# Dequantised FFN weights queued earlier in each group: ternary chunks at 3,3,3,3,3,1,0,0 and 4,4,4,4,2,2,2,0 an iteration

## The chip, the cores and the metric

The kernel runs on the eight cores of one Trainium2 chip. Each core works on eight of the 32 query tiles of one of two batch rows; no core waits for another. Times are device microseconds of the slowest core.

## The reference

One layer: a normalised input goes through a squared-score linear attention and, in parallel, through a feed-forward block whose weights are ternary. Only the second is touched here:

```python
def weight_quant(w):
    scale = 1.0 / jnp.clip(jnp.mean(jnp.abs(w)), 1e-05, None)
    return jnp.clip(jnp.round(w * scale), -1, 1) / scale
def bit_linear(x, w, g):
    xn = rms_norm(x, g)
    xq = ste(xn, activation_quant(xn))
    wq = ste(w, weight_quant(w))
    return xq @ wq.T
y = bit_linear(x, gate_w, gate_norm_w)       # 2048 -> 2 x 5632
gate, up = jnp.split(y, 2, axis=-1)
h = gate * jax.nn.sigmoid(gate) * up
return bit_linear(h, down_w, down_norm_w)    # 5632 -> 2048
```

The output is the input plus the attention plus this block.

## The kernel before

The kernel runs in stages: normalisation and the key, value and query products; the attention; the output product of the attention (L813); the gate/up product; a requantisation of the hidden values; the down product. Between stages all engines meet at a barrier. The change touches the gate/up stage and the down stage.

Weights arrive as float32 and are turned into -1, 0 and 1 on the core, chunk by chunk. A chunk is 128 x 1024 values. `tern_ld` loads two chunks with one DMA of 1 MB on GpSimd's (POOL's) queue into one of two `wfpt` slots; the load waits until both chunks that were last in the slot have been read. `tern_sc` makes a chunk by two signs on ScalarE (L741, L744) and an add on VectorE (L747); its first sign waits for the add of the previous such chunk, since all share `sgn0` and `sgn1`. `tern_dve` makes a chunk on VectorE alone, by two compares and a subtraction (L754, L757, L760).

The gate/up stage has 11 groups `g` of 512 columns and in each 8 row tiles `s`. A group needs 16 chunks, eight for `terng` by `tern_sc` and eight for `ternu` by `tern_dve`, taken alternately. Both weight tiles have two rings: while group g is multiplied, group g+1's chunks are made. In the order of the program, an iteration first queues its chunks (`emit_tern`), then the load of `xqs` for the iteration after next on SyncE (three slots), then 16 matmuls into `gps` (L892) and 16 into `ups` (L904), each over three PSUM slots. After them come the silu on ScalarE (L912), the product `kg2` on VectorE (L916), a square with sum on ScalarE (L921), its accumulation (L925), the weighting (L930), a maximum (L934, L936) and, on SyncE, the store of `hgb` to `hgscr`. `emit_tern(n, max_g=g+1)` stops at the end of group g+1. The first matmul of a group waits for the last chunk of that group; the first chunk of group g+1 waits for the last matmul of group g-1, whose ring it writes.

The down stage has four column blocks `m` of 512 and eight row tiles `s` in each. A block needs 22 chunks, all by `tern_sc`; the chunks of block m+1 are made during block m, those of block 0 in the stage before. An iteration queues its chunks (`emit_dtern`), the load of the next `hqts` (two slots, 1.4 MB) and of `xob` on SyncE, 44 matmuls into `dps` (L1118, two PSUM slots), two steps on VectorE (L1128, and L1134, which reads `xob`), and the store of `outb` on SyncE. The load of `hqts` for s+2 so stands on SyncE's queue behind the store of s.

Every engine works its own instructions off in program order, and the helpers `V` and `SC` make each VectorE and ScalarE instruction also wait for the one before it on its engine.

Of the kernel before, what the change touches and what calls it, by code (L numbers as in the profile page):

```python
# [100 lines left out]
def build_nc():  # L101
# [59 lines left out]
    def SC(fn, waits=(), drain=True):  # L161
        w = list(waits) + ([(cS, cS.n)] if drain else [])
        return b.op("scalar", fn, waits=w, inc=cS)

    def TE(fn, waits=(), inc=True):
        return b.op("tensor", fn, waits=waits, inc=(cT if inc else None))
# [605 lines left out]
    def emit_tern(n, max_g=99):  # L772
        for _ in range(n):
            if tq_i[0] >= len(tern_q):
                return
            kind, g, ring, f2 = tern_q[tq_i[0]]
            if g > max_g:
                return
            tq_i[0] += 1
            extra = [(cT, tern_free[ring])] if (kind == "sc" and f2 == 0) or \  # L780
                    (kind == "dve" and f2 == 0) else ()
            ci = (g * 8 + f2) * 2
            if kind == "sc":
                tern_sc(terng[ring][:, f2 * 1024:(f2 + 1) * 1024],
                        gwt_r, ci, thg_p, thg_m, extra=extra)
            else:
                ck = tern_dve(ternu[ring][:, f2 * 1024:(f2 + 1) * 1024],
                              gwt_r, ci + 1, thg_p, thg_m, extra=extra)
                if f2 == 7:
                    tern_ck_of[g] = (cV.n, cS.n)  # L790
# [73 lines left out]
    for g in range(NPAIR):  # L864
        ring = g % 2
        vck_t, sck_t = tern_ck_of[g]
        tern_ck = vck_t
        for s in range(NOWN):
            pb = (g * NOWN + s) % 3
            it = g * NOWN + s  # L870
            xslot = it % 3
            emit_tern(2, max_g=g + 1)
            if it == 0:
                for ip in (0, 1):
                    b.dma("sync", xqs[ip % 3][:], xqsc[ip % NOWN], s_xq[ip % 3],
                          waits=[(cT, xqs_free[ip % 3])])
            ipre = it + 2
            if ipre < NPAIR * NOWN:
                b.dma("sync", xqs[ipre % 3][:], xqsc[ipre % NOWN],
                      s_xq[ipre % 3], waits=[(cT, xqs_free[ipre % 3])])  # L880
            xq_ck = s_xq[xslot].n
            for fc in range(16):
                wl = []
                if fc == 0:
                    wl = [(s_xq[xslot], xq_ck)]
                    if s == 0:
                        wl += [(cV, tern_ck), (cS, sck_t)]
                    if it < 3:
                        wl += [(cV, ck_wo_v), (cS, ck_wo_s)]
                    en, val = g_ps_free[pb]  # L890
                    wl.append((CTR[en], val))
                TE(lambda e, f=fc, r=ring, bb=pb, xs=xslot: e.matmul(  # L892
                    gps[bb][:], xqs[xs][:, f * 128:(f + 1) * 128],
                    terng[r][:, f * 512:(f + 1) * 512],
                    start=(f == 0), stop=(f == 15)), waits=wl, inc=(fc == 15))
            gck = cT.n
            for fc in range(16):
                wl = []
                if fc == 0:
                    if it < 3:  # L900
                        wl += [(cV, ck_wo_v), (cS, ck_wo_s)]
                    en, val = u_ps_free[pb]
                    wl.append((CTR[en], val))
                TE(lambda e, f=fc, r=ring, bb=pb, xs=xslot: e.matmul(  # L904
                    ups[bb][:], xqs[xs][:, f * 128:(f + 1) * 128],
                    ternu[r][:, f * 512:(f + 1) * 512],
                    start=(f == 0), stop=(f == 15)), waits=wl, inc=(fc == 15))
            uck = cT.n
            xqs_free[xslot] = uck
            if s == NOWN - 1:  # L910
                tern_free[ring] = uck
            sck = SC(lambda e, ss=s, bb=pb: e.activation(  # L912
                kg[:, 0:512], gps[bb][:], ACT.Silu, scale=rsg2[:, ss:ss + 1]),
                waits=[(cT, gck)])
            g_ps_free[pb] = ("cS", sck)
            vck = V(lambda e, ss=s, bb=pb: e.scalar_tensor_tensor(  # L916
                kg2[:, 0:512], ups[bb][:], rsg2u[:, ss:ss + 1], kg[:, 0:512],
                ALU.mult, ALU.mult), waits=[(cS, sck), (cT, uck)])
            u_ps_free[pb] = ("cV", vck)
            aslot = s % 2  # L920
            sck = SC(lambda e, a=aslot: e.activation(  # L921
                kg2[:, 512:1024], kg2[:, 0:512], ACT.Square,
                accum_out=acc_tmp[a][:]),
                waits=[(cV, vck), (cV, acc_free[aslot])])
            V(lambda e, ss=s, a=aslot: e.tensor_add(  # L925
                ssqh[:, ss:ss + 1], ssqh[:, ss:ss + 1], acc_tmp[a][:]),
              waits=[(cS, sck)])
            acc_free[aslot] = cV.n
            hslot = s % 2
            V(lambda e, gg=g, hs=hslot: e.tensor_tensor(  # L930
                hgb[hs][:], kg2[:, 0:512],
                dnw_s[:, gg * 512:(gg + 1) * 512], ALU.mult),
              waits=[(s_hgw[hslot], hgb_free[hslot]), (s_misc, ck_dnw)])
            V(lambda e, hs=hslot: e.reduce_max(lnst[:, 8:9], hgb[hs][:], axis=AX.X,  # L934
                                               apply_absolute_value=True))
            vck = V(lambda e, ss=s: e.tensor_tensor(  # L936
                mxh[:, ss:ss + 1], mxh[:, ss:ss + 1], lnst[:, 8:9], ALU.max))
            b.dma("sync", hgscr[s][:, g * 512:(g + 1) * 512], hgb[hslot][:],
                  s_hgw[hslot], waits=[(cV, vck)])
            hgb_free[hslot] = s_hgw[hslot].n  # L940
# [151 lines left out]
    for it_i, (m, s) in enumerate(it_list):  # L1092
        ring = m % 2
        last_tern = dtern_ck_of[m]
        if True:
            hs = s % 2
            pb = s % 2
            emit_dtern(3, max_m=m + 1)
            if it_i + 1 < len(it_list):
                ns = it_list[it_i + 1][1]  # L1100
                nhs = ns % 2
                b.dma("sync", hqts[nhs][:], hqtd[ns], s_hqt[nhs],
                      waits=[(cT, hqts_free[nhs])])
                hq_ck[nhs] = s_hqt[nhs].n
            b.dma("sync", xob[hs][:],
                  xown[s * 128:(s + 1) * 128, m * 512:(m + 1) * 512],
                  s_xo[hs], waits=[(cV, xob_free[hs])])
            hck = hq_ck[hs]
            xck = s_xo[hs].n
            for fc in range(NFI):  # L1110
                wl = []
                if fc == 0:
                    wl = [(s_hqt[hs], hck)]
                    if s == 0:
                        wl.append((cV, last_tern))
                    en, val = d_ps_free[pb]
                    wl.append((CTR[en], val))
                TE(lambda e, f=fc, h_=hs, bb=pb, r=ring: e.matmul(  # L1118
                    dps[bb][:], hqts[h_][:, f * 128:(f + 1) * 128],
                    dtern[r][:, f * 512:(f + 1) * 512],  # L1120
                    start=(f == 0), stop=(f == NFI - 1)), waits=wl,
                   inc=(fc == NFI - 1))
            hqts_free[hs] = cT.n
            if s == NOWN - 1:
                dtern_free[ring] = cT.n
            mck = cT.n
            ob = s % 2
            vck = V(lambda e, ss=s, mm=m, bb=pb, o=ob: e.scalar_tensor_tensor(  # L1128
                outb[o][:], dps[bb][:], rsd2[:, ss:ss + 1],
                attn_sb[:, ss * DM + mm * 512: ss * DM + (mm + 1) * 512],  # L1130
                ALU.mult, ALU.add),
                waits=[(cT, mck), (s_out[ob], outb_free[ob])])
            d_ps_free[pb] = ("cV", cV.n)
            vck = V(lambda e, o=ob, h_=hs: e.tensor_add(  # L1134
                outb[o][:], outb[o][:], xob[h_][:]), waits=[(s_xo[hs], xck)])
            xob_free[hs] = vck
            b.dma("sync", outd[s * 128:(s + 1) * 128, m * 512:(m + 1) * 512],
                  outb[ob][:], s_out[ob], waits=[(cV, vck)])
            outb_free[ob] = s_out[ob].n
# [101 lines left out]
```

How the kernel before makes its waits and increments, by code:

```python
        def f(eng, wl=wl, fn=fn, ih=ih, inc_n=inc_n, drain=drain):  # L67
            for h, v in wl:
                if v > 0:
                    eng.wait_ge(h, v)
            if drain:
                eng.drain()
            ins = fn(eng)
            if ih is not None:
                ins.then_inc(ih, inc_n)
# [9 lines left out]
        def f(eng, wl=wl):  # L85
            for h, v in wl:
                if v > 0:
                    eng.wait_ge(h, v)
# [6 lines left out]
            def f(eng, h=bar.h, t=target):  # L95
                eng.sem_inc(h, 1)
                eng.wait_ge(h, t)
```

## Time and profile before

| | us |
|---|---|
| timed runs of before | 4507.87 and 4631.96, median 4569.91 |
| profiled execution | 4495.16 |
| its span on the slowest core (7) | 4493.6 |
| spans of the eight cores | 4452.9 to 4493.6 |
| gate/up stage, first to last matmul, core 7 | 3138.5 to 3827 |
| down stage, first to last matmul, core 7 | 4100.5 to 4489 |

The span is measured from the first to the last instruction of a core, in one profiled execution; the profiled execution's own time holds 1.6 us around it. All stages before 3138 us are the same in both kernels. TensorE is busy for 68% of the span, VectorE for 41%, ScalarE for 40%; these are averages over stages and say nothing of what limits one of them. The first of the rows by stage is core 0's down stage, the other two are core 7's gate/up and down stages. In the timeline and the chain, a figure in brackets is the idle time of the engine before that instruction and what ended it.

### The profile page before, as it was taken

The numbers are of one execution on the slowest core, as the hardware profiler recorded it, in microseconds if no ns is written. First come the engines' busy times: TensorE is split into PE (matmuls) and PEld (weight loads), VectorE is DVE, ScalarE is ACT, GpSimd is POOL, SyncE is SP. The second block draws the span as 40 slices with busy tenths as digits, with TensorE's granted clock in tenths as the row PEclk, the third lists the DMA queues.
The fourth block names the chain that finished last, engine by engine and source line by source line (L and its number), as shares of the span: only waits on it lengthen the run. The fifth ranks groups of instructions, "written<-read, shape, count | busy, mean of one in ns | idle before, by whom it ended". The sixth has DMA issues, their size and how long they took to land.

```text
span 4493.6 us, 52826 instructions; the slowest of 8 cores (4452.9 to 4493.6 us)
## 1 busy us (share of the span) xinstructions
PE 3060.2 (68%) x13416; PEld 1284.4 (29%) x13416; DVE 1846.7 (41%) x3416; ACT 1815.7 (40%) x2685; POOL 248.2 (6%) x460
## 2 busy tenths in 40 slices
PE   0776777776776743323277788878988899125999
PEld 0333333332333311111122222223433344012333
DVE  0353443443453433454434322222666665343221
ACT  0333333333333322332256677741444443554550
POOL 1000000000000010000000000000000000000000
PEclk9888887888888866656588899998999999556788
DMA  9434434334434355333222222234667775457884
GB/s 177 118 96 120 114 105 119 105 94 118 117 95 124 109 126 127 103 100 92 75 93 75 100 80 81 81 114 124 221 230 235 233 236 167 160 173 238 272 292 151
DMA packets 326545, 628.24 MB, mean 140 GB/s; under 512 B 199792, under 2 KB 207984, under 8 KB 294256
## 3 DMA queue, kind: packets, MB, share of 16 engines
q0 software_dynamic: 65664, 321.94, 24.7%
q1 hardware_dynamic: 260592, 302.92, 21.5%
q8 instruction: 123, 2.02, 0.2%
q14 instruction: 166, 1.36, 0.1%
HBM read 573.34 MB, written 84.93 MB: 146 GB/s over the span
## 4 chain that ended last, share of the span: by engine, by line
PE 27%; DVE 23%; ACT 14%; DMA 14%; issue 10%; SPq 8%; another core or an unknown queue 3%; DVEq 1%; ACTq 1%; POOL 0%; POOLq 0%
SPq L80 8%; PE kv_ps L357 8%; PE dps L1118 6%; DMA xf<-xfull 5%; ACT s2t L682 3%; PE gps L892 3%; PE ops L688 2%; ACT sgn L741 2%; ACT sgn L744 2%; PE ups L904 2%; ACT s2t L671 2%; DVE kfm L393 2%; DVE lnst L293 2%; PE wops L813 2%
## 5 line engine op out<-in xcount | busy, mean ns | idle before, releaser
L357 PE MATMUL kv_ps<-wk_sb,xnT 128*128 128x512 bf16 x2560 | 653.7, 423 | 199.3 <-DMA wv_sb<-wvt 87.6
L357 PE MATMUL kv_ps<-wv_sb,xnT 128*128 128x512 bf16 x2048 | 481.9, 399 | 87.1 <-DVE kg L367 87.1
L332 PE MATMUL tp_ps<-ident,xnb 128*128 128x128 bf16 x640 | 83.7, 283 | 536.3 <-ACT xnT L338 250.7
L357 PEld LDWEIGHTS kv_ps<-wk_sb,xnT 128*128 128x128 bf16 x2560 | 269.9, 107 | 574.0 <-issue 335.6
L1118 PE MATMUL dps<-dtern,hqts 128*128 128x512 bf16 x1408 | 376.9, 441 | 26.0 <-DMA hqts<-hqtd 25.0
L892 PE MATMUL gps<-terng,xqs 128*128 128x512 bf16 x1408 | 340.1, 398 | 72.8 <-DVE ternu L760 57.1
L673 DVE TENSOR_TENSOR s2t<-s2t,msk_sb 128x512 bf16<-128x512 bf16 x512 | 217.6, 425 | 411.6 <-ACT s2t L671 405.3
L688 PE MATMUL ops<-s2t,vsb 128*128 128x512 bf16 x768 | 303.6, 395 | 103.5 <-DVE s2t L673 76.2
L273 ACT ACTIVATE sgn<-wfp 128x1024 bf16<-128x1024 f32 x264 | 279.0, 1057 | 225.2 <-DMA wfp<-gwt_r 137.4
L671 ACT ACTIVATE s2t<-sps 128x512 bf16<-128x512 f32 x512 | 305.7, 597 | 146.8 <-PE sps L658 116.9
L658 PE MATMUL sps<-qsb,ksb 128*128 128x512 bf16 x768 | 302.2, 398 | 29.1 <-DMA qsb<-qsc 29.0
L904 PE MATMUL ups<-ternu,xqs 128*128 128x512 bf16 x1408 | 318.3, 379 | 0.0
L357 PEld LDWEIGHTS kv_ps<-wv_sb,xnT 128*128 128x128 bf16 x2048 | 206.8, 102 | 362.0 <-issue 147.4
L692 PE MATMUL zps<-s2t,ones_bf 128*128 128x512 bf16 x768 | 304.1, 396 | 0.0
L293 DVE TENSOR_REDUCE lnst<-xf 128x1 f32<-128x2048 f32 x40 | 91.4, 2286 | 436.4 <-DMA xf<-xfull 412.0
L1118 PEld LDWEIGHTS dps<-dtern,hqts 128*128 128x128 bf16 x1408 | 153.6, 110 | 249.1 <-issue 249.0
L418 ACT COPY sgn<-tp_ps 128x512 bf16<-128x512 bf16 x96 | 56.3, 586 | 413.7 <-PE tp_ps L411 218.7
L422 DVE COPY sgn<-tp_ps 128x512 bf16<-128x512 bf16 x96 | 40.8, 425 | 434.2 <-DMA ksc<-sgn 173.5
L892 PEld LDWEIGHTS gps<-terng,xqs 128*128 128x128 bf16 x1408 | 142.3, 102 | 258.2 <-issue 107.6
L332 PEld LDWEIGHTS tp_ps<-ident,xnb 128*128 128x128 bf16 x640 | 53.0, 122 | 562.7 <-issue 559.9
L373 ACT ACTIVATE kg<-kg 128x2048 f32<-128x2048 f32 x40 | 76.4, 1910 | 328.6 <-DVE kg L372 328.6
L290 ACT ACTIVATE xnb<-xf 128x2048 bf16<-128x2048 f32 x40 | 76.4, 1911 | 313.2 <-DMA xf<-xfull 292.3
(139 smaller groups left out, 3540.9 us busy)
## 6 DMA issues: line engine op xcount, KB each, us to landing
wfp<-gwt_r POOLq DMA_DIRECT2D x176, 512.0 KB, 5.2
wfpt<-gwt_r POOLq DMA_DIRECT2D x88, 1024.0 KB, 6.3
wfp<-dwt_r POOLq DMA_DIRECT2D x88, 512.0 KB, 4.7
xqs<-xqsc SPq DMA_DIRECT2D x88, 512.0 KB, 4.6
wfpt<-dwt_r POOLq DMA_DIRECT2D x44, 1024.0 KB, 7.3
hqts<-hqtd SPq DMA_DIRECT2D x32, 1408.0 KB, 8.3
xf<-xfull SPq DMA_DIRECT2D x32, 1024.0 KB, 7.3
hgscr<-hgb SPq DMA_DIRECT2D x88, 256.0 KB, 2.5
```

Source lines behind the costliest of these rows:

```text
L80: return self.op(engine, lambda e, o=out, i=in_: e.dma_start(out=o, in_=i), waits=waits, inc=sem, inc_n=16)
L273: lambda e, sl=slot, t=tgt, cc=col: e.activation(wabs_dump[:], wfp[sl][:], ACT.Abs, accum_out=t[:, cc:cc + 1]), waits=[s_abs[slot]])
L293: V(lambda e: e.reduce_sum(lnst[:, 0:1], xbuf[:], axis=AX.X), waits=[s_x[xslot]])
L357: TE(lambda e, jj=j, f=fc, w=w_sb: e.matmul(kv_ps[jj][:], xnT[:, f * 128:(f + 1) * 128], w[:, f * DM + jj * 512: f * DM + (jj + 1) * 512], ...
L658: TE(lambda e, sl=slot, vv=v, bb=sb: e.matmul(sps[bb][:], ksb[sl][:, vv * 128:(vv + 1) * 128], qsb[sl][:], start=True, stop=True), waits=w ...
L671: sck = SC(lambda e, bb=sb: e.activation(s2t[bb][:], sps[bb][:], ACT.Square), waits=[(cT, mm_ck)])
L673: vck = V(lambda e, bb=sb, vv=v: e.tensor_tensor(s2t[bb][:], s2t[bb][:], msk_sb[:, (vv % 16) * 512:((vv % 16) + 1) * 512], ALU.mult), wait ...
L688: TE(lambda e, sl=slot, vv=v, bb=sb, hh=h, n=NC: e.matmul(ops_[hh % 2][:], vsb[sl][:, vv * 128:(vv + 1) * 128], s2t[bb][:], start=(vv == 0 ...
L692: TE(lambda e, vv=v, bb=sb, hh=h, n=NC: e.matmul(zps[hh % 2][:], ones_bf[:], s2t[bb][:], start=(vv == 0), stop=(vv == n - 1)), inc=(v == N ...
L892: TE(lambda e, f=fc, r=ring, bb=pb, xs=xslot: e.matmul(gps[bb][:], xqs[xs][:, f * 128:(f + 1) * 128], terng[r][:, f * 512:(f + 1) * 512], ...
L904: TE(lambda e, f=fc, r=ring, bb=pb, xs=xslot: e.matmul(ups[bb][:], xqs[xs][:, f * 128:(f + 1) * 128], ternu[r][:, f * 512:(f + 1) * 512], ...
L1118: TE(lambda e, f=fc, h_=hs, bb=pb, r=ring: e.matmul(dps[bb][:], hqts[h_][:, f * 128:(f + 1) * 128], dtern[r][:, f * 512:(f + 1) * 512], st ...
```

## The change

The two calls that queue ternary chunks get another distribution over a group's eight iterations. In the gate/up stage 2 in each iteration becomes 3 in s=0 to 4 and 1 in s=5; the call of 1 in s=6 and 7 finds nothing left that `max_g` lets it take. In the down stage 3 in s=0 to 6 and 1 in s=7 (all that is left) becomes 4 in s=0 to 3 and 2 in s=4 to 6, with nothing left for s=7.

```diff
@@ -869,7 +869,7 @@
             pb = (g * NOWN + s) % 3
             it = g * NOWN + s
             xslot = it % 3
-            emit_tern(2, max_g=g + 1)
+            emit_tern(3 if s < 5 else 1, max_g=g + 1)
             if it == 0:
@@ -1095,7 +1095,7 @@
         if True:
             hs = s % 2
             pb = s % 2
-            emit_dtern(3, max_m=m + 1)
+            emit_dtern(4 if s < 4 else 2, max_m=m + 1)
             if it_i + 1 < len(it_list):
```

## Rows read from the trace of the kernel before

**Rows 1.** Window, length, busy time of PE, PEld, DVE, ACT, POOL; clock; DMA share; GB/s.
```profile
4100.00:4493.00 393.00, 325.02 (x1379) 140.65 (x1406) 91.89 (x130) 151.57 (x132) 16.44 (x31) 0.94 0.75 242
...
3138.50:3829.00 690.50, 631.61 (x2816) 280.03 (x2816) 444.90 (x756) 306.54 (x422) 41.16 (x78) 0.96 0.66 218
4100.00:4493.00 393.00, 376.93 (x1408) 153.55 (x1408) 91.89 (x130) 151.59 (x132) 16.36 (x31) 0.80 0.73 244
```
**Rows 2.** Waits in the gate stage, core 7: total, times, longest.
```profile
PE gps L892 <- DVE ternu L760: 57.1, 10, 6.0
```

**Rows 3.** One gate iteration in order of time, core 7: start, duration, engine.
```profile
3384.07 0.75 DVE L916 SCALAR_TENSOR_TENSOR kg<-ups,rsg2u,kg 128x512 f32<-128x512 f32 x1
3385.03 0.63 ACT L921 ACTIVATE kg<-kg 128x512 f32<-128x512 f32 x1 [3.66 <-DVE kg L916]
...
3385.84 1.15 ACT L741 ACTIVATE sgn<-wfpt,thg_m 128x1024 bf16<-128x1024 f32 x1
...
3387.77 0.16 DVE L936 TENSOR_TENSOR mxh<-mxh,lnst 128x1 f32<-128x1 f32 x1
3388.01 0.32 SPq L80 DMA_DIRECT2D hgscr<-hgb  x1
...
3388.41 0.69 DVE L747 TENSOR_TENSOR terng<-sgn 128x1024 bf16<-128x1024 bf16 x1 [0.47 <-ACT sgn L744]
3388.42 0.43 SPq L80 DMA_DIRECT2D xqs<-xqsc  x1
3389.20 0.75 DVE L754 TENSOR_SCALAR sgn<-wfpt,thg_p 128x1024 bf16<-128x1024 f32 x1
3390.06 0.75 DVE L757 TENSOR_SCALAR sgn<-wfpt,thg_m 128x1024 bf16<-128x1024 f32 x1
...
3391.37 0.53 POOL L80 DMA_DIRECT2D wfpt<-gwt_r  x1 [7.11 <-DVE sgn L757]
3391.72 0.75 DVE L916 SCALAR_TENSOR_TENSOR kg<-ups,rsg2u,kg 128x512 f32<-128x512 f32 x1
...
3391.97 4.96 PE L892 MATMUL gps<-terng,xqs 128*128 128x512 bf16 x16 [5.62 <-DVE ternu L760]
```

**Rows 4.** The chain in the gate stage: first and last group start, one iteration.
```profile
3138.55 5.37 PE gps L892 x16
...
3770.44 5.16 PE gps L892 x16
...
3820.49 3.45 PE gps L892 x16
```

**Rows 5.** Waits in the down stage, core 7.
```profile
PE dps L1118 <- DMA hqts<-hqtd: 25.0, 8, 14.1
```

**Rows 6.** The down stage in order of time, core 7, from its first chunks.
```profile
4109.39 0.69 DVE L747 TENSOR_TENSOR dtern<-sgn 128x1024 bf16<-128x1024 bf16 x1 [22.36 <-ACT sgn L744]
...
4112.79 0.69 DVE L747 TENSOR_TENSOR dtern<-sgn 128x1024 bf16<-128x1024 bf16 x1 [2.71 <-ACT sgn L744]
...
4116.99 0.75 DVE L1128 SCALAR_TENSOR_TENSOR outb<-dps,rsd,attn_sb 128x512 f32<-128x512 f32 x1
...
4119.06 0.98 SPq L80 DMA_DIRECT2D hqts<-hqtd  x1
```

**Rows 7.** VectorE's L1128 in order of time: first and last of block 3.
```profile
4408.78 0.75 DVE L1128 SCALAR_TENSOR_TENSOR outb<-dps,rsd,attn_sb 128x512 f32<-128x512 f32 x1 [10.01 <-PE dps L1118]
...
4489.65 0.75 DVE L1128 SCALAR_TENSOR_TENSOR outb<-dps,rsd,attn_sb 128x512 f32<-128x512 f32 x1 [10.01 <-PE dps L1118]
```

**Rows 8.** Landings in the gate stage: median of `xqs`; range of `wfpt`.
```profile
xqs<-xqsc SPq DMA_DIRECT2D x78, 512.0 KB, 4.6
...
DMA to landing us min/median/max: 4.8/5.9/8.5
```

**Rows 9.** DMA issues in the down stage, with KB and median landing.
```profile
wfpt<-dwt_r POOLq DMA_DIRECT2D x31, 1024.0 KB, 7.6
hqts<-hqtd SPq DMA_DIRECT2D x22, 1408.0 KB, 8.6
```

## The prediction

> **What bounds the kernel now.** I read the profile in this order: the busy time by stage, the waits of the gate stage, one gate iteration in order of time, the chain, the landings, and then the same for the down stage. The change touches two stages, gate/up (3138.5 to 3829 us) and down (4100 to 4493 us).
>
> In the gate stage TensorE looks like the bound: busy 631.6 of 690.5 us at clock 0.96 [rows 1]. But it waits 57.1 us in ten places for the last `ternu` subtraction (L760) [rows 2], and the reader should ask why that one is late. The iteration in order of time tells it [rows 3]. From one `kg2` product (L916, 3384.07) to the next (3391.72) are 7.65 us, and no step of that loop has slack: `kg2`, 0.96 us later the square on ScalarE, 0.81 later the first sign, 2.57 later the add on VectorE, 0.79 later the two compares and the subtraction (2.52 together), then `kg2` again. TensorE needs only 2 x 3.45 = 6.9 us for the same iteration [rows 4]. So a serial ScalarE-VectorE loop sets the pace; TensorE runs ahead by 0.75 us an iteration, and the 5.6 us before 3391.97 are its accumulated lead. Two checks: ten group starts lie between 3138.55 and 3770.44, 63.2 us a group [rows 4], and 8 x 7.65 = 61.2. The missing 2 us come after the pause, where 16 matmuls take 5.4 us and not 3.45 [rows 4].
>
> In the down stage no group of waits has TensorE held by `dtern` on the slowest core; its L1118 matmuls waited 25 us for `hqts` loads [rows 5], which is why a stall at the group change can't be removed there. That core runs this stage at clock 0.80, core 0 at 0.94 [rows 1]. From the L1128 at 4116.99 to that at 4408.78 are 24 iterations with ternary work, 97.3 us for eight; from 4408.78 to 4489.65 seven without, 11.55 us each [rows 6, 7]. 8 x 11.55 = 92.4, so this stage is within 5 us a column block of TensorE's pace.
>
> **The change, part by part.** No instruction is added or removed: 16 chunks a gate group and 22 a down block, the same loads. They are only moved ahead of other work. Gate: 2 in each of 8 iterations becomes 3,3,3,3,3,1,0,0. Down: 3,3,3,3,3,3,3,1 becomes 4,4,4,4,2,2,2,0.
>
> *Gate, the boundary wait.* The last chunk is queued at s=5, so TensorE no longer waits for L760 at the group change. But that wait was the lead over the loop; unless the loop gets shorter, the wait goes elsewhere. So I add up the loop anew, each iteration from its square at 0 [rows 3]; a new sign pair costs 3.40 from add to add [rows 6].
> Iterations with sign, compare, sign chunks (s=0,2,4): add at 3.38, compares beside the next signs, second add at 3.38 + 3.40 = 6.78, `kg2` at 7.58, 8.53 us to the next square.
> Iterations with compare, sign, compare (s=1,3): VectorE is free at 2.98 (after the L936 maximum and its 0.24 us), compare chunk to 5.50, the add to 6.29, second compare chunk to 8.81, 9.76 us in all. The queue behind it is VectorE's own: `kg2`, and behind `kg2` the square.
> s=5: 2.98 + 2.52, 6.45 us. s=6,7: 3.93 us each.
> Sum: 3 x 8.53 + 2 x 9.76 + 6.45 + 2 x 3.93 = 59.4 us. That would beat 63.2 (two engines overlap better), but two queues get in the way.
>
> *The weight loads on POOL's queue.* Two slots hold two chunks each. A slot's reload is issued 1.31 us after the L757 compare starts [rows 3] and lands 5.9 us later, 4.8 to 8.5 [rows 8]; so 7.3 us after that compare starts. Today the pair is wanted later than that. With three chunks an iteration it isn't hidden: pair 2 can start its signs at 8.53 + 0.81 = 9.3 but is there at 5.03 + 7.3 = 12.3; its add comes at 14.9 and not at 14.0. Carried on through the group, pairs 4, 5 and 7 come about 0.4 us late each: 2.2 us in all. At a landing of 4.8 the sum of these is 0; each further microsecond beyond 5.9 costs about 3 us a group, so at 7.6, the median that the same load has in the down stage [rows 9], it is 7.3 us.
>
> *SP's queue.* The `xqs` load for iteration it+3 stands on SyncE behind the store of `hgscr` of it. The store goes 3.94 us after `kg2` (3388.01), the load 0.41 later [rows 3], it lands in 4.6 [rows 8], and 6.9 us of matmuls follow: `kg2` of it+3 can't come earlier than 15.9 us after `kg2` of it. Today three iterations take 22.9 and nobody notices. After the change s=5, 6 and 7 take 6.45 + 2 x 3.93 = 14.3, so the light iterations are held 1.6 us, and the loop can't catch up.
>
> Group: 59.4 + 2.2 + 1.6 = 63.2 us, what it is today. Over the ten groups that carry chunks the gain is therefore nil at the median landing: the first `kg2` comes 0.9 later, and the last group starts without the slow matmuls (-2). I take 0. At 4.8 the group is 61.0: -22 us; at 7.6 it is 68.3: +51.
>
> Here the trace meets the Trainium skill. "DMA: Bandwidth & Descriptors", section "Issuing engines are not separate DMA queues", says that transfers issued from different engines share the same 16 DMA engines and interleave. The trace agrees where the load slows from 5.9 to 7.6 us beside the down stage's loads [rows 8, 9]. The page's table of measured bandwidth gives 6.15 us for 1 MB; by that figure alone the gate stage would come out some 8 us longer than my sum.
>
> *Down.* A sign chunk costs 3.40 us, add to add [rows 6]; the first of an iteration hides its signs. From one L1128 to the next with four: 1.65 (the two `outb` steps) + 3 x 3.40 + 0.8 = 12.7 us. But a slot of two chunks is in use for 3.40 + 2.4 us and then reloads in 0.6 + 7.6 [rows 9]: 14.0 us, and four chunks need both slots. So 14.0 an iteration at s<4, and 13.7 for the first, whose signs wait for the ring. The `hqts` load for s+2 is queued on SP behind the store of s: 2.07 us after L1128 (4116.99 to 4119.06) [rows 6], 8.6 to land [rows 9], 11.6 of matmuls: 22.3 us from evacuation to evacuation over two. From the last evacuation of a block at 0: s=0..3 at 13.7, 27.7, 41.7, 55.7; s=4 at 41.7 + 22.3 = 64.0; s=5 at 55.7 + 22.3 = 78.0; s=6, 7 at 89.6 and 101.2. Against 97.3 that is 4 us a block, 12 us for three blocks. With 12.7 for 14.0 it is 0; with 16, for a landing of 9.6, about 30.
>
> **Sum.** The profiled execution took 4495.16 us, 1.6 more than its span of 4493.6. 4495 + 0 + 12 = 4507 us. The two timed runs of before were 4507.87 and 4631.96; the forecast is for undisturbed runs, of the kind of the first, and is no change against them. 2% (90 us) is about what a measurement of this kernel can tell from none.
>
> **Rivals.**
> R1, the loads stay short (4.8 us) and the down stage pays nothing: 4495 - 22 = 4473 us. For it: today's load already has the DMA engines at 0.66 of their time in the gate stage [rows 1], so there is room. Against it: the extra loads are bunched where `xqs` and `hgscr` also run. Chance 0.20.
> R2, slower: the weight loads set the pace of the heavy iterations. Place: the two slots behind POOL's queue. Price: 3 us a group for each microsecond of landing above 5.9, so at 7.6 +51, and with +12 to +20 below: 4560 us; at 6.7 it is 4531. It decides over everything else from 6.3 us on, where it costs 12 us, as much as the down stage. For it: 7.6 in the down stage at share 0.73 [rows 1, 9]. Chance 0.18.
> R3, slower: the clock. If the gate stage fell to the 0.80 that core 7 has below [rows 1], 32 matmuls would take 32/44 x 11.55 = 8.4 us, more than the loop, 88 x 8.4 = 739 against 690 now: +49, with the down stage 4556 us. "TensorE: Matmul & The Clock Gate", section "Seeing it yourself", of the Trainium skill says that a die whose cores run dense matmuls is held at 13/16 of the clock; TensorE would be no denser here by my sum, and the trace shows 0.96 [rows 1]. Chance 0.06.
> R4, TensorE really runs free in the gate stage: 88 x 6.9 = 607 against 690: -83, with the down stage 4424 us. Against it stands the whole loop [rows 3]. Even this is less than 2%. Chance 0.03.
>
> **How the numbers follow.** My own case, both stages within a few loads of the sum (4485 to 4530), gets 0.50 and gives 4507 us. R1 0.20, R2 0.18, R3 0.06, R4 0.03, other mishaps 0.03. The range goes from R1 (4473, less 3) to R2's end (4560, plus 5): 4470 to 4565; outside are R4, the rest, and part of R3, about 0.1. Faster by over 2% (under 4405) would need more than R4: 0.01. Slower by over 2% (over 4585) needs R2's upper end with a bad down stage, or R2 and R3 together: 0.05. Within: 0.94.
>
> **What would show it.** After: no group TensorE `gps` <- VectorE `ternu`; in its place TensorE waiting for `xqs` or for L912/L916 in the middle of groups; ScalarE signs (L741) with waits for `wfpt` in the middle of the gate stage; intervals of L916 in the pattern 8.5, 9.8-10.6, 8.9, ..., 6.5, 4, 5.5; eight adding to about 63. In the down stage L1128 intervals of 14 us at s=1..3. I am wrong if the eight add to 60 or less (then a queue did not bind), if the landing exceeds 6.5 us, or if down blocks stay at 97.

## The result and the profile after

The changed kernel is slower: 4551.39 us (median of 12 runs, 4519.0 to 4651.54) against 4488.94 us for the kernel before (median of 11, 4479.1 to 4631.96). The ratio is 1.0114, with a 95% interval of 1.0077 to 1.0151, some 51 us; executions in which one die ran at a lower clock are left out of the ratio but not of the medians, which is why these lie further apart. In the profiled executions the spans of the slowest core are 4493.6 and 4542.8 us.

Where the time came from is best read from one instruction per iteration: L916 in the gate stage and L1128 in the down stage, on all eight cores. I use two measures all through this part. The group period is the time from the L916 of iteration 7 to that of iteration 79, divided by 9. A block is the time from the first L1128 of a column block to that of the next. Both are means over the cores. Differences between kernels are taken from these means before rounding. Where a profile had cores at a clearly lower granted clock (the mean TensorE clock that the profile shows for a stretch, 1.00 being the upper of its two levels), they are named.

| | group period | down blocks 0, 1, 2 | gate + down against before |
|---|---|---|---|
| before | 63.1 | 100.2, 98.5, 94.3 | |
| after | 66.1 | 107.0, 111.3, 98.3 | +27, +24 |

For the gate stage, 9 x 3.0 = 27 us and 2.4 more in group 0, which the period leaves out, less 2.8 us in the last group, which has no chunks and lost the pause at its start. For the down stage 6.8 + 12.8 + 4.0 = 24 us. Together 50 us; the stretches in which both kernels do the same (up to the gate stage, between the two stages, block 3) happen to be 5 us shorter. The spans of the eight cores differ by 45 us in the mean, those of the slowest by 49.

Waits of the changed kernel in the gate stage from 3200 to 3740 us, core 7 (waiting instruction, releaser: total us, times, longest):

```profile
ACT sgn L741 <- DMA wfpt<-gwt_r: 58.2, 28, 4.4
...
PE gps L892 <- DMA xqs<-xqsc: 48.2, 21, 5.1
...
PE gps L892 <- ACT kg L912: 11.3, 3, 5.5
```

The wait for the last `ternu`, 57.1 us over the whole stage in [rows 2], is gone, exactly as the change is written to do. TensorE now waits in three other places: for its `xqs` load, for the silu that has to free a PSUM slot, and, through ScalarE, for the weight loads. The L916 of one group, in order of time on the same core, show the rhythm:

```profile
3417.02 0.75 DVE L916 SCALAR_TENSOR_TENSOR kg<-ups,rsg2u,kg 128x512 f32<-128x512 f32 x1 [1.63 <-PE ups L904]
3425.60 0.75 DVE L916 SCALAR_TENSOR_TENSOR kg<-ups,rsg2u,kg 128x512 f32<-128x512 f32 x1 [0.16 <-DVE terng L747]
3436.76 0.75 DVE L916 SCALAR_TENSOR_TENSOR kg<-ups,rsg2u,kg 128x512 f32<-128x512 f32 x1
3447.16 0.75 DVE L916 SCALAR_TENSOR_TENSOR kg<-ups,rsg2u,kg 128x512 f32<-128x512 f32 x1 [0.16 <-DVE terng L747]
3456.95 0.75 DVE L916 SCALAR_TENSOR_TENSOR kg<-ups,rsg2u,kg 128x512 f32<-128x512 f32 x1
3467.60 0.75 DVE L916 SCALAR_TENSOR_TENSOR kg<-ups,rsg2u,kg 128x512 f32<-128x512 f32 x1
3474.08 0.75 DVE L916 SCALAR_TENSOR_TENSOR kg<-ups,rsg2u,kg 128x512 f32<-128x512 f32 x1
```

Intervals of 8.6, 11.2, 10.4, 9.8, 10.6 and 6.5 us. Over all cores and groups the eight are 8.6, 10.7, 9.8, 10.5, 9.8, 6.5, 4.0 and 6.1; before they were 9.5 at s=0, behind the pause, and 7.6 to 7.7 at the other seven.

One place, in order of time, shows what a late load does. A slot is freed by the compare at 3423.01, its reload is issued at 3424.32, and ScalarE, whose next instruction needs it, stands idle for 3.6 us until 3430.89. Behind that sign stand the next sign and the silu (L912), and only then the add and the product:

```profile
3423.01 0.75 DVE L757 TENSOR_SCALAR sgn<-wfpt,thg_m 128x1024 bf16<-128x1024 f32 x1
...
3424.32 0.53 POOL L80 DMA_DIRECT2D wfpt<-gwt_r  x1 [16.57 <-DVE sgn L757]
...
3430.89 1.15 ACT L741 ACTIVATE sgn<-wfpt,thg_m 128x1024 bf16<-128x1024 f32 x1 [3.61 <-DMA wfpt<-gwt_r]
...
3432.13 1.15 ACT L744 ACTIVATE sgn<-wfpt,thg_p 128x1024 bf16<-128x1024 f32 x1
3433.37 0.69 ACT L912 ACTIVATE kg<-gps,rsg 128x512 f32<-128x512 f32 x1
3433.45 0.69 DVE L747 TENSOR_TENSOR terng<-sgn 128x1024 bf16<-128x1024 bf16 x1 [1.47 <-ACT sgn L744]
```

The same happens in the down stage, most of all at the start of block 1. Here with four chunks in an iteration the reload issued at 4258.40 is first read at 4268.18, 9.8 us later, and the one issued at 4267.18 at 4276.90, 9.7 us later:

```profile
4258.40 0.53 POOL L80 DMA_DIRECT2D wfpt<-dwt_r  x1 [22.11 <-ACT sgn L744]
...
4265.21 0.75 DVE L1128 SCALAR_TENSOR_TENSOR outb<-dps,rsd,attn_sb 128x512 f32<-128x512 f32 x1
...
4267.18 0.53 POOL L80 DMA_DIRECT2D wfpt<-dwt_r  x1 [8.26 <-issue]
...
4268.18 1.15 ACT L741 ACTIVATE sgn<-wfpt,thd_m 128x1024 bf16<-128x1024 f32 x1 [3.95 <-DMA wfpt<-dwt_r]
...
4276.90 1.15 ACT L741 ACTIVATE sgn<-wfpt,thd_m 128x1024 bf16<-128x1024 f32 x1 [2.93 <-DMA wfpt<-dwt_r]
...
4283.66 0.75 DVE L1128 SCALAR_TENSOR_TENSOR outb<-dps,rsd,attn_sb 128x512 f32<-128x512 f32 x1
```

From 4265.21 to 4283.66 are 18.5 us for one iteration. TensorE had that result at 4272.5, but its evacuation (L1128, which reads it out of PSUM) stands on VectorE behind the four adds.

The second of these loads is a special one. Its slot is free at 4264.24 and it is issued 2.9 us later, where most need 0.55. It is the 26th of the down stage's 44 weight loads, and in the kernel before, in the changed one and in `e2_down_only` below it is issued 2.95 us late on all eight cores; why, no run here shows. In the changed kernel it then goes out at the same moment as an `hqts` load (0.07 us apart on seven cores, 0.47 on one) and takes 9.2 to 13.0 us to land. The iteration of a core is longer by just what this landing is longer: 18.5 us with 9.2, 20.5 with 11.3, 22.2 with 13.0. In e2 one core has the two loads 1.06 us apart: there it lands in 5.3 us and the iteration takes 16.2.

### The profile page after: what moved, and what is told of

Its sections match the earlier page's. It is cut to its first block, busy times and chain, and to the rows that moved or that the text cites. A ratio compares the mean times of both kernels' runs of the same rounds, so it can differ in the third digit from the quotient of the medians.

```text
span 4542.8 us, 52826 instructions; the slowest of 8 cores (4479.9 to 4542.8 us)
## 1 busy us (share of the span) xinstructions
PE 3040.5 (67%) x13416; PEld 1274.2 (28%) x13416; DVE 1846.7 (41%) x3416; ACT 1815.7 (40%) x2685; POOL 248.2 (5%) x460
## 4 chain that ended last, share of the span: by engine, by line
PE 26%; DMA 19%; DVE 18%; ACT 16%; issue 9%; SPq 8%; another core or an unknown queue 3%; DVEq 1%; ACTq 1%; POOL 0%; POOLq 0%
PE kv_ps L357 10%; SPq L80 7%; DMA xf<-xfull 5%; DMA wfpt<-gwt_r 4%; ACT s2t L682 3%; PE gps L892 3%; PE dps L1118 3%; ACT sgn L741 3%; ACT sgn L744 3%; PE ops L688 2%; PE ups L904 2%; ACT s2t L671 2%; DVE lnst L293 2%; PE wops L813 2%
## 5 line engine op out<-in xcount | busy, mean ns | idle before, releaser
L357 PE MATMUL kv_ps<-wv_sb,xnT 128*128 128x512 bf16 x2048 | 498.3, 409 | 101.4 <-DVE kg L367 101.4
L1118 PE MATMUL dps<-dtern,hqts 128*128 128x512 bf16 x1408 | 337.2, 404 | 76.1 <-DMA hqts<-hqtd 69.9
L1118 PEld LDWEIGHTS dps<-dtern,hqts 128*128 128x128 bf16 x1408 | 143.2, 103 | 269.9 <-issue 127.1
```

The lines of the kernel that those rows point to most:

```text
L357: TE(lambda e, jj=j, f=fc, w=w_sb: e.matmul(kv_ps[jj][:], xnT[:, f * 128:(f + 1) * 128], w[:, f * DM + jj * 512: f * DM + (jj + 1) * 512], ...
L1118: TE(lambda e, f=fc, h_=hs, bb=pb, r=ring: e.matmul(dps[bb][:], hqts[h_][:, f * 128:(f + 1) * 128], dtern[r][:, f * 512:(f + 1) * 512], st ...
```

## The experiments

Three theories stood at the start. T, that of the prediction: bunched chunks run into two queues, the weight slots behind POOL and the `xqs` load behind the store on SyncE, in both stages. D or G: one stage carries the whole loss. V: three chunks in an iteration overload VectorE and ScalarE, and the queues only fill gaps.

### Each half alone

`e1_gate_only` has the first hunk of the change, `e2_down_only` the second. `e11_gate_again` is e1 once more.

> Only the gate/up calls are changed (3,3,3,3,3,1,0,0); the down stage is that of before. Theory T (both halves of the change cost time, each through a queue): in the changed kernel the gate groups take about 66 us against 63.2 of before, so this kernel is 25 to 30 us slower than before (ratio 1.006). Rival D (the down stage carries the whole loss): ratio 1.000. Rival G (the gate stage carries it all): ratio 1.011.

> Only the down calls are changed (4,4,4,4,2,2,2,0); the gate stage is that of before. T: column blocks of 107, 111 and 98 us where before has 99 to 104, 98 and 93 on the cores with the fast clock: 20 to 25 us slower (ratio 1.005). D: ratio 1.011. G: ratio 1.000.

> The same kernel as e1 (gate change alone), whose timed runs gave no interval. 80 gate iterations took 648 us there against 626: T expects 20 to 25 us slower than before, ratio 1.005, which with the 1.0067 of the down change alone makes up the 1.0114 of both. Rival: ratio 1.000 (the trace showed one bad execution).

e1's profile has a group period of 65.9 us and down blocks of 100.0, 98.5 and 93.6, those of before; its timed runs gave no interval. The second run of the same kernel gave one: 1.0089 (1.0046 to 1.0131), group period 66.7. Cores 4 and 5 had a clock of 0.82 in that gate stage and 68.1 and 67.4 us, the other six lie at 65.7 to 67.1. e2 gives 1.0067 (1.0032 to 1.0103), with blocks of 104.2, 109.4 and 100.8 and a gate stage of 63.1 to 63.2 us on six cores (4 and 5 had 0.90 and 0.89 and are left out). So both halves cost time, about as much each, and D and G fall. The two ratios add to more than the 1.0114 of both, but within their intervals. By the traces the last 80 gate iterations cost 22 us in e1 and 27 on those six cores of e11, and 24 in the changed kernel; the down stage costs 21 in e2, and 24 in the changed kernel.

### The two queues of the gate stage

`e3_gate_slot3` gives the loads a third slot. Two idle buffers of 1024 columns, `wfp[0]` and `wfp[1]`, serve as one:

```diff
-        slot = (i // 2) % 2
+        slot = (i // 2) % 3
...
+            else:
+                b.dma("gpsimd", wfp[0][:], src_r[:, ci * 1024:(ci + 1) * 1024],
+                      s_gw[slot], waits=wl)
+                b.dma("gpsimd", wfp[1][:],
+                      src_r[:, (ci + 1) * 1024:(ci + 2) * 1024], s_gw[slot])
```

`e4_gate_xq4` keeps two slots, but has four `xqs` buffers and loads three iterations ahead:

```diff
-            ipre = it + 2
+            ipre = it + 3
...
-            xslot = it % 3
+            xslot = it % 4
```

`e5_gate_both` has both. All three have the gate half of the change and the down order of before. The third slot serves the down stage too, since both stages load through `tern_ld`; what it does there by itself comes below.

> As e1, but with a third slot for the weight loads (two buffers that lie idle in these stages), so that a reload has a pair's time more to land. T (the loads behind POOL's queue make the groups long): ScalarE's waits for wfpt inside the gate stage go from 64 us to under 10, the groups from 66 to about 62 us; 35 to 45 us faster than e1, ratio to before about 0.997. Rival V (bunching three chunks on two engines costs the time by itself, the loads only fill gaps): the group stays at 65 to 66 and the ratio at that of e1.

> As e1, but with a fourth xqs slot, each load issued one iteration earlier, so that it stands one store earlier on SyncE. T (the xqs load behind the store holds the light iterations): TensorE's waits for xqs go from 56 us to about 0, the L916 intervals at the end of a group from 6.5, 4.0, 5 to 8 to 6.5, 4.0, 4.0; the group 1.5 to 2.5 us shorter, 15 to 25 us faster than e1. Rival L (what is gained there is lost to the weight loads, which then come closer together): as e1.

> As e1, with the third slot for weight loads and the fourth xqs slot together. The last 80 gate iterations took 626 us in before, about 648 with the gate change alone (e1), 613 with the third slot (e3), 624 with the fourth xqs slot (e4). T (two independent queues on top of a ScalarE-VectorE loop of 59.4 us a group): the two gains add, 648 - 35 - 24 = 589 to 596 us, which is the loop alone; 30 us faster than before, ratio 0.992 or less. Rival S (both take away the same wait): about 610, as e3.

| | group period | intervals of L916, s=0 to 7 | ratio to before |
|---|---|---|---|
| e1 | 65.9 | 8.6, 10.6, 9.9, 10.4, 9.8, 6.5, 4.0, 6.0 | see e11: 1.0089 |
| e3, third weight slot | 62.0 | 8.6, 9.9, 8.6, 9.8, 8.6, 6.5, 4.0, 5.9 | 0.9943 (0.9897 to 0.9990) |
| e4, fourth `xqs` slot | 63.8 | 8.6, 10.7, 9.7, 10.6, 9.8, 6.5, 4.0, 4.0 | 1.0023 (0.9991 to 1.0055) |
| e5, both | 60.1 | 8.6, 9.9, 8.6, 9.8, 8.6, 6.5, 4.0, 4.0 | 0.9844 (0.9786 to 0.9902) |

The third slot shortens the iterations with three chunks and leaves the last one at 5.9; the fourth `xqs` buffer shortens the last one to 4.0 and leaves the others. The effects, 3.9 and 2.0 us a group, add to 5.9, and e5 is 5.8 shorter than e1. Over the last 80 iterations e3 is 35 us shorter than e1 and e4 24, both within what was expected, and e5's 591 us lie where T put them. So S falls, since the gains add, and L, since e4 keeps its gain. One detail was missed: in e4 TensorE's waits for `xqs` go from 62.3 us in e1 to 28.8 (core 7), and not to about 0. V falls with e3: the engines do the same work in the same order and the group is 3.9 us shorter. In e5's waits from 3200 to 3740 us, core 7, the loads of weights are gone from the list of what anybody waits for, and of TensorE's 48.2 us for `xqs` are left

```profile
PE gps L900 <- DMA xqs<-xqsc: 15.5, 11, 4.3
```

which cost nothing, since the ScalarE-VectorE loop and not TensorE sets the pace. One group of e5, from the same instruction as above (there L924), repeats to the hundredth:

```profile
3413.82 0.75 DVE L924 SCALAR_TENSOR_TENSOR kg<-ups,rsg2u,kg 128x512 f32<-128x512 f32 x1
3422.40 0.75 DVE L924 SCALAR_TENSOR_TENSOR kg<-ups,rsg2u,kg 128x512 f32<-128x512 f32 x1 [0.16 <-DVE terng L755]
3432.20 0.75 DVE L924 SCALAR_TENSOR_TENSOR kg<-ups,rsg2u,kg 128x512 f32<-128x512 f32 x1
3440.78 0.75 DVE L924 SCALAR_TENSOR_TENSOR kg<-ups,rsg2u,kg 128x512 f32<-128x512 f32 x1 [0.16 <-DVE terng L755]
3450.58 0.75 DVE L924 SCALAR_TENSOR_TENSOR kg<-ups,rsg2u,kg 128x512 f32<-128x512 f32 x1
3459.16 0.75 DVE L924 SCALAR_TENSOR_TENSOR kg<-ups,rsg2u,kg 128x512 f32<-128x512 f32 x1 [0.16 <-DVE terng L755]
```

8.58, 9.80, 8.58, 9.80, 8.58: the prediction's 8.53 and 9.76 with no wait in them.

### Is the third slot a gain by itself?

> The kernel before with the third slot for weight loads and nothing else. Theory T says that at two chunks an iteration the loads are covered and the serial loop paces the gate stage: 80 gate iterations stay at 626 us, ratio 0.998 to 1.001. Rival F (the third slot is a gain of its own, and e3, e5 and e6 showed that and not the loads of the bunched order): 600 to 615 us and ratio 0.990 or less.

In the profile of `e8_before_slot3` the group period is 63.0 to 63.3 us on six cores (2 and 3 had 0.91 there, and 64.4 and 64.2 us), against 63.1, and the blocks are 99.5, 98.5 and 94.6, against 100.2, 98.5 and 94.3. Its timed runs gave no interval, so only the trace speaks: with two chunks an iteration in the gate stage and three in the down stage, two slots are enough. F falls.

### The down stage

`e6_down_slot3` is e2 with the third slot.

> As e2 (down change alone), with the third slot for weight loads. T (four chunks an iteration wait for two slots, 14.0 us for 12.7): blocks of 103 to 110 us come back to 96 to 100, ratio to before 1.000. Rival Q (hqts behind the later stores on SyncE, or the DMA engines themselves, set the down stage): blocks stay at 103 to 110, ratio 1.006.

Ratio 0.9976 (0.9933 to 1.0018), blocks 100.8, 102.5 and 94.7. Against e2 (104.2, 109.4, 100.8) that is 3.4 + 6.9 + 6.1 = 16 of the 21 us; 5 us are left over before. T had expected blocks of 96 to 100. These 5 us can't be told from nothing: in the ten profiles whose down stage has the order of before, the three blocks add up to 289 us (e7) to 303 (e4), with 293 in before; e6 has 298, and e2 and the changed kernel, with 314 and 317, lie outside. The L1128 (there L1136) intervals of block 1, mean over the cores, from s=0:

| | s=0 | 1 | 2 | 3 | 4 | 5 | 6 | 7 |
|---|---|---|---|---|---|---|---|---|
| before | 14.2 | 10.7 | 15.1 | 10.9 | 12.9 | 11.6 | 12.6 | 11.1 |
| after | 14.2 | 20.5 | 13.7 | 15.8 | 8.5 | 15.2 | 10.7 | 12.6 |
| e2 | 13.5 | 20.4 | 13.9 | 15.2 | 8.2 | 15.9 | 10.8 | 11.2 |
| e6 | 13.7 | 13.6 | 13.9 | 14.0 | 9.5 | 13.7 | 12.6 | 10.7 |

The 20.5 belongs to block 1 alone: in blocks 0 and 2 of the changed kernel s=1 takes 13.7 and 15.5 us. The four-chunk iterations of e6 take 13.6 to 14.0 us in every block (s=1 to 3): that is about 4 x 3.40, the chain of sign, sign, add. I had expected 12.7, taking the first pair of signs as hidden behind the evacuation. Since e6 also has more instructions on POOL's queue, and no weight load in its down stage is issued 2.95 us late, what it gains at s=1 of block 1 is not all shown to be the slot's. Q, that `hqts` or the DMA engines set the stage, holds for the small rest at most.

### The whole change with wider queues

> The whole change (3,3,3,3,3,1,0,0 and 4,4,4,4,2,2,2,0) with the third weight slot and the fourth xqs slot. T: gate 591 us as in e5, down blocks as in e6 (101, 103, 95), together 30 to 35 us faster than before, ratio 0.984 to 0.988, where the change without them is 1.0114. Rival C (with both stages bunched and more loads in flight the DMA engines saturate): ratio 0.995 or more.

`e12_after_wide` is the changed kernel with the third weight slot and the fourth `xqs` buffer. Ratio 0.9906 (0.9860 to 0.9952), group period 60.1, blocks 100.9, 101.7 and 93.9. The profile is what T said; the ratio is somewhat less good than the 0.984 to 0.988 expected, and the upper end of the interval reaches C's 0.995, but no mean interval in the gate stage is longer than in e5, so there is no saturation to be seen. The same change that costs 1.1% gains about 0.9% once the two loads it presses have room.

### Opening the loop itself

If the serial loop of [rows 3] is the pace of the kernel before, the better cure is to break it. `e7_late` starts from the kernel before and queues the chunks not at the head of the iteration but behind the `kg2` product and ahead of the square, so that ScalarE makes its signs while VectorE still works on the last ones:

```diff
-            emit_tern(2, max_g=g + 1)
...
             u_ps_free[pb] = ("cV", vck)
+            vck_kg = vck
+            emit_tern(3 if s < 2 else (2 if s < 7 else 0), max_g=g + 1)
...
-                waits=[(cV, vck), (cV, acc_free[aslot])])
+                waits=[(cV, vck_kg), (cV, acc_free[aslot])])
```

The numbers change with the place: 3,3,2,2,2,2,2,0, so that the last chunk is still made in time. `e9_late_xq4` adds the fourth `xqs` buffer, `e10_late_xq4_slot3` the third slot too.

> The kernel before with the gate chunks queued behind the kg2 product (and ahead of the square) and not at the head of the iteration, 3,3,2,2,2,2,2,0 of them. If the serial loop kg2, square, signs, add, compares is what paces the gate stage of before, this opens it: VectorE then has 6.3 us of work an iteration and no wait for signs, TensorE 6.9. Expected: L916 intervals of 6.9 in the two-chunk iterations, 80 iterations in 565 to 590 us against 626, 35 to 60 us faster than before (ratio 0.987 to 0.992). Rival V (VectorE and ScalarE are held by something else, the loads for instance): 620 or more.

> As e7 with the fourth xqs slot. The store of hgscr now stands some 2.5 us later behind kg2, so xqs behind it may bind in e7: if it does, e7 shows waits of TensorE for xqs and this kernel takes them away, 80 iterations in 553 (TensorE's own pace) to 570 us, ratio about 0.985; if not, as e7.

> As e9 (gate chunks queued behind kg2, 3,3,2,2,2,2,2,0, four xqs slots), with the third weight slot. e9 took 568 us for 80 gate iterations, and its three-chunk iterations 10 and 8.5 us. T: these fall to 8.8 and 7.1, and the stage comes to TensorE's own pace, 553 to 560 us; ratio to before 0.978 to 0.982. If the loads don't matter there, as e9 (0.983).

| | group period | intervals, s=0 to 7 | ratio to before |
|---|---|---|---|
| e7 | 60.8 | 7.0, 7.3, 10.2, 7.9, 7.3, 7.1, 7.0, 7.0 | 0.9948 (0.9900 to 0.9996) |
| e9 | 57.1 | 5.6, 7.3, 10.6, 7.8, 6.4, 6.4, 6.5, 6.6 | 0.9830 (0.9754 to 0.9906) |
| e10 | 55.3 | 6.9, 7.3, 8.8, 6.3, 6.4, 6.3, 6.4, 6.9 | 0.9805 (0.9735 to 0.9875) |

The chunks queued in iteration s now fall into the interval that ends at s+1. With them late, the intervals of e7 with two chunks take 7.0 to 7.3 us, and 7.9 right behind those with three, where before had 7.65; so the serial loop was the pace, and V's 620 us or more fall. But e7 gained less than expected: 603 us for the last 80 iterations, not 565 to 590, and a ratio of 0.9948, not 0.987 to 0.992. Two queues hold it: on core 7 up to 3740 us TensorE waits 52.5 us for `xqs` and ScalarE 68.2 us for the weights. With the fourth buffer (e9, 568 us) the two-chunk intervals away from the heavy ones are 6.4 to 6.6 us. With the third slot too (e10, 552.5 us, at the lower end of what was expected) the longest goes from 10.6 to 8.8, and the group comes to 55.3 us on every core, which is 8 x 6.9, the matmuls and nothing else: TensorE is busy for all of the stretch from 3300 to 3600 us on core 7. The intervals of e9's and e10's ratios overlap; that the slot helps is read from the traces. Three places of e10's gate stage on core 7, with the wait for TensorE back where it belongs:

```profile
3414.08 0.75 DVE L923 SCALAR_TENSOR_TENSOR kg<-ups,rsg2u,kg 128x512 f32<-128x512 f32 x1 [0.43 <-PE ups L911]
3420.98 0.75 DVE L923 SCALAR_TENSOR_TENSOR kg<-ups,rsg2u,kg 128x512 f32<-128x512 f32 x1 [0.73 <-PE ups L911]
3427.89 0.75 DVE L923 SCALAR_TENSOR_TENSOR kg<-ups,rsg2u,kg 128x512 f32<-128x512 f32 x1 [3.05 <-PE ups L911]
```

e10 beats both kernels: its ratio to before is 0.9805, that of the changed kernel 1.0114.

## Why the prediction was right and wrong

It forecast 4507 us, 12 more than the profiled execution, and called that no change. Measured are 51 us more. What failed are sizes, and one term that was put at nothing. The step that failed most is the cost of the weight loads behind their two slots: 2.2 us a group in the gate stage, where 3.9 were measured, and 14.0 us for a four-chunk iteration of the down stage, where those at s=1 to 3 took 15.5 in the mean. Left out was TensorE's lower clock behind the new waits for `xqs`. The loop of the two engines and which queues would bind were right. Four sizes were off to the same side, so that they added up.

*The loop in the kernel before* (right). That TensorE's 57 us were its lead over a ScalarE-VectorE loop, and that removing the wait would not return them, is shown by e5 (the wait is gone, the pace is the loop, and what is gained is only that the loop of the bunched order is 3.0 us a group shorter) and e7 to e10 (open it, and the time is there).

*The loop of the changed order*, forecast 59.4 us a group. e5 measures 60.1. Off by 0.7: every one of the eight intervals is 0.03 to 0.14 us longer than my sums, most of them by 0.05, with some 0.3 us longer.

*The weight loads*, forecast 2.2 us a group at a landing of 5.9. e1 less e3 gives 3.9. The slope, 3 us a group for a microsecond of landing, held. In 144 groups of the changed kernel and e1, the five heavy iterations took 2.4 us more than in e5 where the loads landed in 5.7 us in the mean (18 groups), and 5.5 us more where they landed in 6.8 (19 groups); the prediction's line gives 1.7 and 4.9. So 0.6 us are missing at any landing, whose cause stays open; the rest is the landing, which was read on one core. The slowest core had the shortest but one of the eight. The same line of the DMA issues of before, in the gate stage, on cores 0, 4 and 5:

```profile
wfpt<-gwt_r POOLq DMA_DIRECT2D x68, 1024.0 KB, 6.5
...
wfpt<-gwt_r POOLq DMA_DIRECT2D x68, 1024.0 KB, 6.6
...
wfpt<-gwt_r POOLq DMA_DIRECT2D x69, 1024.0 KB, 7.1
```

The eight are 6.5, 5.7, 6.4, 6.4, 6.6, 7.1, 6.1 and 5.9, mean 6.3, and in the changed kernel it is 6.3 again (6.0 to 6.4). With 6.3 the sum gives 2.2 + 3 x 0.4 = 3.4, against 3.9 measured. This number was in the trace of before. A sum over loads in a stage in which all cores run the same code should have used the landing of all of them, the more so as the prediction itself named 6.3 as the point from which this decides.

*The `xqs` load*, forecast 1.6 us a group, measured 2.0 (e1 less e4). The last interval has a mean of 6.1 and not 5.5, though the load that it waits for lands in 4.1 us in the mean and not in 4.6. What the sum left out is TensorE's clock. Behind a wait of 4.5 us its matmuls start slowly, as after the pause of before, which the prediction had in its rows and put at nothing here. The end of the group shown above:

```profile
3477.25 4.91 PE L892 MATMUL gps<-terng,xqs 128*128 128x512 bf16 x16 [4.48 <-DMA xqs<-xqsc]
3482.00 3.62 PE L904 MATMUL ups<-ternu,xqs 128*128 128x512 bf16 x16
...
3485.80 0.75 DVE L916 SCALAR_TENSOR_TENSOR kg<-ups,rsg2u,kg 128x512 f32<-128x512 f32 x1 [3.90 <-PE ups L904]
```

The granted clock is 0.61 from 3477.2 to 3480.7 us and 1.00 from there to 3485.5. In the 144 last intervals of the changed kernel and e1, 105 have 1.00 over their first 3.45 us of matmuls: there it is 7.24 us from TensorE's start to L916, and the interval is 5.5 in the mean, as forecast (by luck in part: the load landed in 4.0 us there). In the other 39 it is 0.56 in the mean, mostly the lower level (1.2 of 2.4 GHz); TensorE had stood still for 3.3 us in the mean against 1.0, and the interval is 7.6.

Together: 59.4 + 2.2 + 1.6 = 63.2 was forecast, and 60.1 + 3.9 + 2.0 = 66.0 is what the experiments give; the profile has 66.1. Each half microsecond is multiplied by nine groups, and group 0 takes 2.4 us more besides.

*The ends of the stage*. The last group was forecast 2 us shorter and is 2.8 shorter; the first `kg2` was forecast 0.9 us later and is 0.2 later.

*The down stage*, forecast 12 us, measured 24. In kind it was as forecast: four-chunk iterations paced by the slots, a short one at s=4, and `hqts` behind a later store at s=5. But 14.0 us were forecast for each of the nine iterations at s=1 to 3, and they took 15.5 in the mean, 14 us in all, which is more than the miss. Half of it, 6.5 us, is the one iteration of 20.5 us, whose reload took 2.95 us to be issued and 11.3 to land in the mean, where the sum has 0.6 and 7.6. The delay of this load was in the trace of before, where it costs nothing visible (10.7 us for that iteration). The other eight took 14.9 us; the reloads of the heavy iterations landed in 8.0 us in the mean. With a third slot all nine take 13.6 to 14.0. The yardstick, a core at clock 0.80 with 97.3 us a block, did no harm: the mean of the eight cores was 97.7.

*The rivals.* R2, the weight loads set the pace, is what happened, halfway: at a landing of 6.3 us its rule, 3 us per group and microsecond, puts the gate stage 12 us over my sum. R1 and R4 fell. Of R3, a gate stage held at 0.80, the profile has nothing: the stage's clock is 0.94 on core 7, against 0.96. And by the figure of 6.15 us for 1 MB in the Trainium skill ("DMA: Bandwidth & Descriptors", the table of measured bandwidth, which is of a single core) the sum would have been nearer than by the row I used, though still short: the eight cores' mean is 6.3.

That the time lies within 4470 to 4565 us says little for the forecast: the range was wide enough for R1 and R2 both, and what was forecast was no change.

## What to carry to other kernels

When a fast engine waits for a slow pair at a group change, look whether the wait is a late item or the lead of an engine that runs ahead of a serial loop; in the second case moving the item moves the wait. Before bunching work, follow each of its loads: how long the slot is in use, how long the reload takes on all cores, what else goes out with it, and what stands behind it on its queue. Each new wait that stops the fast engine for microseconds can cost it clock besides. The real cure was the order within an iteration (work of the next item between the two halves of this one) with one more buffer on each queue that this presses.

## What the runs showed of the hardware

The lower clock can hold for two cores of a die and not for its other two. Before's down stage (4100 to 4493 us), cores 5 and 6, in the columns of [rows 1]:

```profile
4100.00:4493.00 393.00, 316.53 (x1369) 136.22 (x1367) 91.17 (x129) 147.07 (x128) 16.36 (x31) 0.94 0.70 235
...
4100.00:4493.00 393.00, 352.13 (x1303) 143.59 (x1327) 87.66 (x124) 141.01 (x123) 15.34 (x29) 0.81 0.70 232
```

A 1 MB load that went out with a 1.4 MB load within 0.07 us landed in 9.2 to 13.0 us on seven cores of the changed kernel. POOL mostly issued a load 0.55 us after its slot was free; one load of the down stage was issued 2.95 us after it in the same place of the program, on all eight cores of three kernels.
